# Delta rule: the levels on the chunks' own blocks of 32 columns, all tiles together, on parts of the array

## The reference

```python
def _delta_rule_chunkwise(q, k, v, beta, chunk=32):
    q, k = _l2norm(q), _l2norm(k)
    v, kb = v * beta[..., None], k * beta[..., None]
    # qc, kc, vc, kbc: q, k, v, kb cut into chunks of 32 tokens
    M = where(strict_lower, kbc @ kc^T, 0)          # 32x32 in each chunk and head
    T = solve_triangular(eye + M, eye, lower=True)  # (1 + M)^-1
    u, w = T @ vc, T @ kbc
    def step(S, (q_i, k_i, u_i, w_i)):              # over the 8 chunks of a sequence
        attn = where(incl_lower, q_i @ k_i^T, 0)
        u_adj = u_i - w_i @ S
        out_i = q_i @ S + attn @ u_adj
        S = S + k_i^T @ u_adj
```

## Time and profile before

| | us |
|---|---|
| median of 3 runs | 3085.36 (3081.5 to 3087.89) |
| the profiled execution | 3082.87 |
| its span, first to last instruction | 3081.5 |

### The profile page before, as it was taken

The page is one execution under the profiler, slowest core; times in us unless marked ns, Lnnn a source line. Parts: engine busy times, 40 slices in busy tenths (PEclk is TensorE's granted clock), DMA queues, the critical chain, the costliest instruction groups (busy, mean ns, idle before and its releaser), DMA issues. The chain is left out here.

```text
span 3081.5 us, 41110 instructions
## 1 busy us (share of the span) xinstructions
PE 2574.1 (84%) x15734; PEld 1687.9 (55%) x15734; DVE 2116.9 (69%) x4051; ACT 1415.8 (46%) x2561; POOL 553.4 (18%) x482
## 2 busy tenths in 40 slices
PE   5889897885878688989788877879878989879889
PEld 1257674553666324757555557659755455455554
DVE  6988888988998999998789776660264142452331
ACT  5533336884542453333388664340134344334342
POOL 2710001226780064000022037000010000000100
PEclk8899899996986688999899888769989999989999
DMA  3000001110000000000111200009300000000000
GB/s 154 0 1 1 1 1 28 42 42 4 1 1 1 0 1 0 1 1 34 70 41 42 79 1 1 1 1 276 100 1 1 0 1 1 7 1 1 1 2 7
DMA packets 51924, 73.18 MB, mean 24 GB/s; under 512 B 5776, under 2 KB 41360, under 8 KB 51088
## 3 DMA queue, kind: packets, MB, share of 16 engines
q1 hardware_dynamic: 51728, 70.56, 7.6%
HBM read 52.32 MB, written 1.44 MB: 17 GB/s over the span
## 5 line engine op out<-in xcount | busy, mean ns | idle before, releaser
L146 PEld LDWEIGHTS ps<-held_ffn,hidden 128*128 128x128 f32 x2304 | 300.2, 192 | 145.9 <-issue 117.8
L164 ACT ACTIVATE grown<-ps,bias_grown 128x512 f32<-128x512 f32 x288 | 197.9, 687 | 317.1 <-PE ps L146 315.8
L146 PE MATMUL ps<-held_ffn,hidden 128*128 128x128 f32 x2304 | 306.1, 276 | 11.8 <-DVE hidden L183 11.8
L177 POOL TENSOR_TENSOR qk<-conv,held_const 128x512 f32<-128x512 f32 x64 | 90.1, 1408 | 936.7 <-DVE conv L183 936.7
L183 DVE SCALAR_TENSOR_TENSOR conv<-conv_in,held_l1a,conv 128x512 f32<-128x512 f32 x288 | 238.7, 848 | 16.0 <-ACT conv L164 12.9
L177 POOL TENSOR_TENSOR long<-long,product 128x512 f32<-128x512 f32 x136 | 191.9, 1450 | 156.4 <-ACT product L164 154.8
L183 DVE SCALAR_TENSOR_TENSOR hidden<-ps,bias_kept,grown 128x512 f32<-128x512 f32 x288 | 214.7, 748 | 6.8
L177 POOL TENSOR_TENSOR part<-state,c_rows 128x512 f32<-128x512 f32 x128 | 162.4, 1293 | 88.1 <-issue 47.4
L180 DVE TENSOR_SCALAR grown<-grown,bias_fallen 128x512 f32<-128x512 f32 x288 | 138.5, 482 | 53.5 <-ACT grown L164 47.7
L207 POOL MEMSET wide_q<- 128x1536 f32 x8 | 11.0, 1378 | 912.9 <-DVE stream_b L180 863.1
L146 PE MATMUL ps<-part,held_const 128*128 128x512 f32 x256 | 157.4, 721 | 7.4 <-POOL part L177 5.6
(11 more groups left out here) (442 smaller groups left out, 5610.7 us busy)
## 6 DMA issues: line engine op xcount, KB each, us to landing
ring<-lags SPq DMA_DIRECT2D x64, 512.0 KB, 4.7
turned<-conv SPq DMA_DIRECT2D x256, 64.0 KB, 2.0
held_ffn<-in_ffn SPq DMA_DIRECT2D x1, 4690.0 KB, 19.0
held_l1a<-in_l1a SPq DMA_DIRECT2D x2, 2120.0 KB, 15.9
held_l3f<-in_l3f SPq DMA_DIRECT2D x1, 2824.0 KB, 12.2
held_rows<-in_rows SPq DMA_DIRECT2D x1, 1044.5 KB, 8.4
out<-x SPq DMA_DIRECT2D x4, 256.0 KB, 2.6
held_const<-in_const SPq DMA_DIRECT2D x1, 785.0 KB, 4.7
```

The costliest lines, as they stand in the source:

```text
L146: ins = self.real.matmul(out, lhsT, rhs, **kw)
L164: return self.sent(self.real.activation(out, a, func, **kw), 0.13 + columns(out) / 1150, 0.14)
L177: return self.vector(self.real.tensor_tensor(out, a, b, op), columns(out), out, a, b)
```

## The change

1. The three masks are stored as 32 columns instead of 128.
2. `placed` happens once for all four tiles, early (before the norms of q and k), straight from PSUM; kb is copied beside it by ACT (`placed_k`) instead of DVE. PE's transposes of kb wait for `placed`, since they reuse its bank.
3. `mix` makes only the 32x32 blocks, for all tiles together, and q k^T with them: 3 x 4 tiles x 4 chunks x 4 heads = 192 small matmuls for a stream. DVE masks the three results in one instruction each (`masked`).
4. A level works on all tiles, in two halves (one sequence each, `q`). `blocks` issues, for 2 tiles, 4 heads and 4 chunks, 32x32 matmuls at array positions (32c, 32c): 32 for each half of the power, 32 for each of its transpose, 32 (64 columns) for the right side. ACT copies both powers of a half in one instruction; DVE only adds.
5. The last level writes u and w apart, so that `w_tok` goes; w is transposed from there. The wait for the long filter, its transposes and ACT's copy move behind the scan and `mixed`, which is made of 32x32 blocks as well; the gate's first ACT instruction waits for that copy.
6. The planner: another cost for f32 matmuls with a tile position, and `lead`, which lets the stream that is ahead yield a little while both are in layers 8 to 10 (the start of the second pass).

```diff
@@ Lane.matmul
         r, c = kw["tile_position"]
+        if lhsT.dtype == F32:
+            cost = max(n / 600, 0.03 + lhsT.shape[-1] / 660)
@@ Weave
+    def lead(self, rank):
+        mine, other = self.finished[rank], self.finished[3 - rank]
+        n = min(len(mine), len(other))
+        if n not in self.catch_up:
+            return 0.0
+        if len(mine) > n:
+            return max(0.0, max(e.free for e in self.engines.values()) - mine[n])
+        return max(0.0, other[n - 1] - mine[n - 1]) if len(other) == n else 0.0
...
-                    key = (max(ready, e.free + 0.5), lane.rank == BEHIND, ready, lane.rank)
+                    late = 0.05 * self.lead(lane.rank) if lane.rank in self.finished else 0.0
+                    key = (max(ready, e.free + 0.5), lane.rank == BEHIND, ready + late, lane.rank)
@@ delta_rule, tensor
         for t in range(NT):
-            if t:
-                yield pe.wait_ge(s.added, LEVELS * t)
-                yield pe.wait_ge(s.squaredT_kept, (LEVELS - 1) * t)
-            for k, (left, right) in enumerate(((b.kbn, b.kn), (b.kn, b.kbn))):
+            for k, (left, right) in enumerate(((b.kbn, b.kn), (b.kn, b.kbn), (b.kn, b.qn))):
+                for c_ in range(PER):
+                    at = slice(P * t + CH * c_, P * t + CH * c_ + CH)
+                    for h in range(H):
+                        r = slice(D * h, D * h + D)
+                        mm = pe.matmul(st.ps(h)[block(c_), P * k + CH * t:P * k + CH * t + CH], left[r, at], right[r, at],
+                                       start=True, stop=True, tile_position=(D * h, CH * c_), skip_group_check=True)
+        mm.then_inc(s.mix)
+        def blocks(q, out, left, right):
+            for t in range(TPS * q, TPS * q + TPS):
                 for h in range(H):
...
+                    for c_ in range(PER):
+                        mm = pe.matmul(out(t - TPS * q, h)[block(c_), :], left(t, h)[block(c_), :],
+                                       right(t, h)[block(c_), :], start=True, stop=True,
+                                       tile_position=(CH * c_, CH * c_), skip_group_check=True)
+            return mm
+        for i in range(LEVELS):
+            y_, n_of = y[i % 2], lambda k: lambda t, h: n[i % 2][:, t, k, block(h)]
+            for q in range(SEQS):
+                square = lambda k: lambda t, h: st.tiles(2 * q + 1)[:, 2 * t + k, block(h)]
                 if i == 0:
...
+                    yield pe.wait_ge(s.placed, 1)
+                    yield pe.wait_ge(s.placed_k, 1)
+                    yield pe.wait_ge(s.masked, 3)
                 else:
...
+                    yield pe.wait_ge(s.squares_kept, SEQS * (i - 1) + q + 1)
+                if i < LEVELS - 2:
+                    blocks(q, square(0), n_of(1), n_of(0))
                 if i < LEVELS - 1:
...
+                    blocks(q, square(1), n_of(0), n_of(1)).then_inc(s.squares)
+                if i:
+                    yield pe.wait_ge(s.added, SEQS * (i - 1) + q + 1)
+                blocks(q, lambda t, h: st.ps(2 * q)[:, 2 * D * (H * t + h):2 * D * (H * t + h + 1)], n_of(1),
+                       lambda t, h: y_[:, H * t + h, :]).then_inc(s.applied)
...
-        yield pe.wait_ge(s.long, LONG - BY_VECTOR)
-        for t in range(NT):
-            mm = pe.transpose(st.tiles(1)[:, t, :], tile(b.long, t), m.ident)
-        mm.then_inc(s.long_turned)
         yield pe.wait_ge(s.wT_kept, 1)
-        yield pe.wait_ge(s.long_kept, 1)
...
         mm.then_inc(s.mixed)
+        yield pe.wait_ge(s.long, LONG - BY_VECTOR)
+        for t in range(NT):
+            mm = pe.transpose(st.tiles(1)[:, t, :], tile(b.long, t), m.ident)
+        mm.then_inc(s.long_turned)
+        yield pe.wait_ge(s.long_kept, 1)
@@ delta_rule, scalar
+        for i in range(LEVELS - 1):
+            k = 0 if i < LEVELS - 2 else 1
+            for q in range(SEQS):
+                yield act.wait_ge(s.squares, SEQS * i + q + 1)
+                act.activation(n[(i + 1) % 2][:, of_pair(q), k:, :],
+                               st.ps(2 * q + 1).rearrange("p (t k c) -> p t k c", t=TPS, k=2)[:, :, k:, :], ACT.Copy
+                               ).then_inc(s.squares_kept)
@@ delta_rule, vector
+        yield ve.wait_ge(s.beta, 1)
+        yield ve.wait_ge(s.turned_v, 1)
+        ve.tensor_tensor(y[0][:, :, 0:D], grouped(st.tiles(2)), beta, ALU.mult).then_inc(s.placed)
...
+        yield ve.wait_ge(s.mix, 1)
+        for k, (out, kept) in enumerate(((by_head(n[0][:, :, 0, :]), w.minus_low), (by_head(n[0][:, :, 1, :]), w.minus_high),
+                                         (by_head(mixT), w.upto))):
+            ve.tensor_tensor(out, by_bank(k), mask(kept), ALU.mult).then_inc(s.masked)
...
+                of = slice(G // 2 * q, G // 2 * q + G // 2)
+                src, out = y[i % 2][:, of, :], st.ps(2 * q).rearrange("p (g d) -> p g d", d=2 * D)
+                if i < LEVELS - 1:
+                    ve.tensor_tensor(y[(i + 1) % 2][:, of, :], src, out, ALU.add).then_inc(s.added)
```

More of the change, by code:

```diff
@@ L1294, in delta_rule @@
               "filtered turned_qk turned_v taken taken_v squared sums shifted_n root normed kb turned_again taken_again "
-              "turned_f taken_f placed low_kept high_kept mix applied added squaredT squaredT_kept squared_n squared_kept "
-              "product long attended mix_kept "
-              "w_tok w_turned long_turned long_kept wT_kept ws adj qs gain state mixed qs_kept out "
+              "turned_f taken_f placed placed_k masked mix applied added squares squares_kept "
+              "product long "
+              "w_turned long_turned long_kept wT_kept ws adj qs gain state mixed qs_kept out "
               "mean mean_kept size sq0 middled sq1 l2_in l2 var stat_turned stat_copied up hidden "
@@ L1587, in vector @@
-                ve.tensor_tensor(half(dst), half(src), two[:, :, :, 0:2 * D], ALU.add).then_inc(s.added)
-        yield ve.wait_ge(s.added, LEVELS * NT)
-        L.past(ve, "placed low_kept high_kept squared_kept added")
-        yield ve.wait_ge(s.long, LONG - BY_VECTOR)
-        ve.tensor_copy(grouped(f.w_tok[:, :, :]), e.y[:, :, :, D:2 * D].rearrange("p t h d -> p (t h) d")
-                       ).then_inc(s.w_tok)
-        yield ve.wait_ge(s.attended, 1)
-        for h in range(H):
-            ve.tensor_tensor(f.mixT[:, :, h, :], st.tiles(h), w.upto.unsqueeze(1).to_broadcast([P, NT, P]), ALU.mult
-                             ).then_inc(s.mix_kept)
+                    yield ve.wait_ge(s.placed, 1)
```

141 lines of the change are left out of this document (53 added, 88 removed).

## The result

The changed kernel takes 3110.5 us (median of five runs, 3103.1 to 3118.2) against 3085.7 (five runs of the kernel before, beside it): the ratio is 1.0088, 95% interval 1.0068 to 1.0108. It is **slower by 0.9%**; I had predicted 2994 us and gave slower one chance in ten. The profiled execution took 3118.2 us, 35.4 more than the profiled one of before.

The account below looks back on a forecast made before the run. A chain of PE, DVE and ACT in the levels, with waits for POOL, was taken as the bound. Gains of 49.5 us (round 2) and 46 (round 1), less 4 for orders, gave 91.5: 2994 us, range 2952 to 3065.

Parts of the forecast that it names:

- What bounds the kernel: Both rounds: the levels' chain, DVE placements waiting for POOL, and a scan that begins only after the long filter.
- DVE: Masks, placements and additions in the levels: 17 us less for each stream, plus the waits for POOL; memsets 0.17 us.
- PE: Mix and levels on small parts: levels of both streams 42 us against 112 in round 2, mix 3 us.
- ACT's order: ACT's fixed order in the levels: products wait for POOL, copies stand behind products; 6 us of stalls, before 21.9.
- the first rival: Levels outpace ACT and POOL but the clock falls, or ACT's order adds POOL's stalls: 3040 us, chance 0.18.
- the second: Rival: parts writing one bank take turns, levels 140 us for both streams: 3155 us; chance 0.13 with slow issue.
- The planner: New matmul cost and lead: another order here and there, no sum, 4 us either way.
- The long filter: Moved from the front of the scan, it is late next; POOL's 68 additions take 84.3 us in round 2.
- Sums: Whole kernel: 49.5 us from round 2 and 46 from round 1, less 4 for orders, 91.5 gained: 2994 us.
- The clock: Levels were put at 2.4 GHz; a rival had 1.2 GHz, levels 70 to 75 us and scan 33.

Follow-up runs that it names:

- e6: e3 with merged matmuls, 704 instead of 960 for mix and levels: 3019.8 us, ratio 0.9800 to the kernel before.
- e9: e6 with DVE instead of PE making the transposed powers, 448 matmuls: 3004.9 us, ratio 0.9744 to the kernel before.
- e13: e9 with the long filter's transposes and ACT's copy in front of the scan again: 3061.7 us, ratio 0.9916 to the kernel before.
- e1: A kernel of its own issuing long runs of matmuls: 512 f32 32x32 over four parts took 27.5 us in one bank, 26.6 in four.
- e5: The changed kernel with the planner of before, neither the new cost nor lead: 3066.0 us, ratio 0.9951 to the kernel before.
- e2: The kernel before with the planner's two changes alone: 3108.7 us, ratio 1.0076 to the kernel before.
- e3: The changed kernel, planned at 0.058 us instead of 0.016 for a small f32 matmul: 3065.0 us, ratio 0.9938 to the kernel before.
- e12: e4 with the long filter's transposes and ACT's copy in front of the scan again: 3056.6 us, ratio 0.9909 to the kernel before.
- e4: The changed kernel with levels on whole 128x128 matrices again and the planner of before: 3068.8 us, ratio 0.9958 to the kernel before.
- e15: e9 without lead: 2999.0 us, ratio 0.9707 to the kernel before.

## Why the prediction was wrong

*What bounds the kernel* was right in two of its three parts: shorter levels (e6, e9) and the filter behind the scan (e13 against e9) made the kernel faster. What DVE's placements behind POOL cost, no run tested by itself.

*DVE* was right. I had 17 us for each stream and round, 68, and the waits; DVE is busy 97 us less. The state's memsets take 0.165 us each, where I took 0.17. In the changed kernel they all fell into gaps of POOL; that an addition beside them costs nothing shows in e9 (at 849, 853, 1836 and 1840 us, POOL busy throughout).

*PE* is **the step that failed**. It had 42 us for the levels of both streams and 3 for the mix; they take 111, because PE's instructions come at 256 in 3.7 us. I worked out an array time (0.035 and 0.060 us a record on its part) from the 52 records of q k^T and a spacing from four starts in 0.03 us. Both rows are true, and neither is long enough: in e1 446 instructions ran before the first pause, so only a longer run of small ones shows the supply. I had 11 to 40 us a stream as bounds; the upper one, 0.026 us a record "as if that rate were a limit of issue", was near the truth (0.029) for a reason that I did not have. By my own sum the kernel is slower than before "once a record costs over" 0.029 us, and this is where it came to lie. The number that would have told was in the diff: 1920 x 4 instructions in place of some 780 records of PE and as many of PEld. Six packets of instructions in 112 us became thirty in 111.

*ACT's order* I charged with 6 us of stalls of POOL. There were 75 in round 2. Two of my rivals name parts of it: the first ("ACT's order makes POOL's stalls add to the levels") has the mechanism with the wrong size, since I took the levels at 70 to 75 us; the second has the size (0.029 us a record "or slowly issued") with the wrong mechanism (e1: no turns).

*The planner* was **the other step that failed**: "no sum; 4 us either way". I compared old and new cost for one kind only, a part of 32 or 64 columns with a right side of 128, and did not work it out for the 32x32 parts that the change brings in, where it falls from 0.056 to 0.020 us a matmul. e5 against the changed kernel makes it 44 us. Even the tiny differences of the other shapes cost the kernel before 20 us (e2).

*The long filter* leaving the front of the scan was right in kind: it is last in both rounds, its 68 additions take 84.1 us without stalls where I had 84.3 (e3), and the kernel with the move is 57 us faster in e9 against e13. On whole matrices it showed no gain (e12 against e4), and in the changed kernel itself it was not tested.

*Sums.* e9 has the levels about as short as I had predicted (mix and levels in 59 us), with 14 packets instead of 30 and a plan that knows the rate: its gate begins at 909.5 where I had 912, and in round 2 86 us after POOL's first addition where I had 92. It takes 3005 us against my 2994. It is another kernel, though, so that the two are near does not make the prediction right. The 111 us between the changed kernel (3110) and e15 (2999) go, as the runs are ordered, in 45 for the planned rate (e3), 45 for eight packets (e6), 15 for eight more (e9) and 6 for lead (e15); by the ratios 46, 43, 17 and 11. *The clock* was low in the levels (0.60 in 1842 to 1953), as the first rival had it, but it was not what set their length: e1 has the same pace at 0.50. In A's and B's scan of round 2 the clock was 0.50 and the stretch 27 us; in e3 the stretch of 25 us that holds the scan ran at 1.00 after levels at 0.55. What decides between these two no run here tells apart.

## What to carry to other kernels

Count instructions, not only columns: when many small matmuls stand in a row, multiply them by four for f32 (two for bf16), divide by 256 and take 3.7 us for each; small parts run at their own pace only from about 0.015 us of work an instruction (3.7/256), or in runs of less than some 450. Merging matmuls that share an operand and giving transposes of 32x32 blocks to DVE gained 60 us here, the parts by themselves nothing (e5 against e4). Where a planner fixes the orders, its costs are part of the kernel: a cost that is too low by three made ACT and DVE stand behind PE and took away 45 us, so set it from the trace, and try an edit under more than one plan before you believe a difference under 20 us.

## What the runs showed of the hardware

- PE's instructions come in packets of 16,384 B (256 instructions), one each 3.7 us when PE waits for them: in a kernel that does nothing else (e1, bursts 3.45 to 4.00 us apart, clock 0.50) as beside all other engines (30 in 111 us, clock 0.60). A transfer takes about 1.1 us of that. Less than two packets lay ready (a first burst of 446 instructions in e1).
- Four 32x32 f32 parts that write one bank, each on its own partitions, run together: 15 ns a record at 1.2 GHz (e1), about 9 at 2.4 (60 records of the changed kernel's levels in 0.74 us, below, at a clock of 1.00 in 1938.3 to 1951.8); one part alone takes 54 ns at 1.2 GHz.

```profile
1938.93 0.74 PE L146 MATMUL ps<-n_odd 32*32 32x32 f32 x60
```

- A f32 matmul on the whole array with only 32 columns takes 109.4/256 = 0.43 us at 1.2 GHz. With 128 columns it takes 31.0/128 = 0.24 us at 0.92, so that it is not the columns that bound the smaller one (e1).
- DVE turns 32x32 blocks out of PSUM at nearly the rate of a copy: 256 columns in 0.45 us (16 in e9's round 2) against 0.42 (`outT<-ps` of the kernel before), and it did not stand behind POOL's additions.
